# The D term of two state-space scans: from a matmul with a diagonal to a transpose of scaled rows, at every second state

## The reference

```
A_bar = exp(dt[t, d] * A[d, n])
h[t, d, n] = A_bar * h[t-1, d, n] + dt[t, d] * B[t, n] * x[t, d]
y[t, d] = sum over n of h[t, d, n] * C[t, n]  +  D[d] * x[t, d]
```

## Time and profile before

| What | us |
|---|---|
| median of 3 runs | 686.62 |
| lowest and highest run | 686.56, 692.63 |
| span of the profiled execution, first to last instruction | 657.3 |
| PE busy in the span | 602.7 (92%) |
| DVE busy | 530.2 (81%) |
| ACT busy | 513.7 (78%) |
| POOL busy | 429.1 (65%) |
| scan of layer 0, start of the first and of the last full recurrence | 49.35, 201.82 |
| scan of layer 1, the same | 282.08, 432.86 |

### The profile page before, as it was taken

One profiled execution on the slowest core, in us unless ns is written; L12 is line 12 of the kernel. 1 busy time (PEld: TensorE's weight loads), 2 busy tenths in 40 slices (PEclk: granted clock), 3 DMA queues, 4 the chain that ended last, 5 costly groups with the idle time before them and its releaser, 6 DMA issues.

```text
span 657.3 us, 12812 instructions
## 1 busy us (share of the span) xinstructions
PE 602.7 (92%) x4540; PEld 501.7 (76%) x4543; DVE 530.2 (81%) x899; ACT 513.7 (78%) x1182; POOL 429.1 (65%) x261
## 2 busy tenths in 40 slices
PE   5898999999996569799999999999999999999992
PEld 3388999999996434599999999989677555555662
DVE  6798999999998789989999999987863566555374
ACT  2999999999995798899999999967544665444335
POOL 0037999999999302479999999995004277777403
PEclk8979999999999699999999999999999999999997
DMA  7022333333331000044544454438112133333173
GB/s 198 6 67 65 112 112 105 108 109 114 103 110 32 2 0 7 19 147 134 180 128 153 145 159 155 147 91 274 43 64 65 33 97 97 97 99 96 56 265 128
DMA packets 41596, 67.78 MB, mean 103 GB/s; under 512 B 6688, under 2 KB 20928, under 8 KB 41536
## 3 DMA queue, kind: packets, MB, share of 16 engines
q1 hardware_dynamic: 37696, 56.50, 27.5%
q0 software_dynamic: 3840, 10.49, 5.1%
HBM read 57.28 MB, written 9.70 MB: 102 GB/s over the span
## 4 chain that ended last, share of the span: by engine, by line
PE 57%; DVE 14%; ACT 13%; POOL 8%; DMA 4%; issue 3%; DVEq 1%; SPq 0%; ACTq 0%; POOLq 0%
PE both L1383 16%; PE bank L1412 12%; POOL arena L1184 7%; PE both L1476 7%; PE both L1385 5%; PE both L1463 4%; PE bank L1483 4%; DMA arena<-w 2%; ACT rings L1045 2%; PE bank L1404 2%; DVE arena L658 2%; DVE st L443 1%; PE bank L1584 1%; ACT rings L923 1%; ACT tok_a L996 1%
## 5 line engine op out<-in xcount | busy, mean ns | idle before, releaser
L1184 POOL TENSOR_TENSOR arena<-arena,rings 128x1024 f32<-128x1024 f32 x126 | 296.8, 2375 | 17.5 <-DVE arena L658 13.4
L1383 PE MATMUL both<-rings,tok_a 128*128 128x128 f32 x1280 | 183.3, 277 | 3.6 <-DVE arena L658 2.2
L1383 PEld LDWEIGHTS both<-rings,tok_a 128*128 128x128 f32 x1280 | 164.6, 193 | 5.1 <-issue 2.9
L658 DVE TENSOR_TENSOR_SCAN arena<-rings,both 128x1024 f32<-128x1024 f32 x64 | 145.3, 2279 | 12.3 <-PE both L1385 4.5
L658 DVE TENSOR_TENSOR_SCAN arena<-late,both 128x1024 f32<-128x1024 f32 x62 | 140.7, 2278 | 7.1 <-PE both L1385 1.8
L1412 PE MATMUL bank<-ident,arena 128*128 128x128 f32 x1024 | 133.0, 273 | 2.8 <-POOL arena L1184 1.4
L1412 PEld LDWEIGHTS bank<-ident,arena 128*128 128x128 f32 x1024 | 115.7, 141 | 4.2 <-POOL arena L1184 1.9
L1045 ACT ACTIVATE rings<-ident,b_tok 128x128 f32<-128x128 f32 x320 | 106.6, 394 | 0.3
L1045 ACT ACTIVATE rings<-tok_a,b_tok 128x256 f32<-128x256 f32 x192 | 89.7, 500 | 0.0
L1385 PE MATMUL both<-ident,rings 128*128 128x128 f32 x384 | 84.0, 273 | 0.0
L1199 POOL TENSOR_TENSOR arena<-arena,feat_a 128x512 f32<-128x512 f32 x8 | 19.4, 2425 | 86.2 <-DVE arena L554 86.2
(11 more groups left out here) (233 smaller groups left out, 1045.9 us busy)
## 6 DMA issues: line engine op xcount, KB each, us to landing
rings<-c_rows SPq DMA_DIRECT2D x128, 256.0 KB, 3.2
w_sb<-w SPq DMA_DIRECT2D x18, 352.0 KB, 4.2
arena<-w SPq DMA_DIRECT2D x2, 2048.0 KB, 13.2
residual<-x SPq DMA_DIRECT2D x4, 512.0 KB, 5.8
x_rows<-tok_a SPq DMA_DIRECT2D x4, 512.0 KB, 2.6
tok_a<-y_tok SPq DMA_DIRECT2D x4, 512.0 KB, 6.3
w_sb<-y_tok SPq DMA_DIRECT2D x4, 512.0 KB, 7.0
out<-residual SPq DMA_DIRECT2D x8, 256.0 KB, 2.6
```

The source lines that it names most:

```text
L658: dve.tensor_tensor_scan(h_s, decay_s.rearrange("p h t -> p (h t)"), both[s % B_RING][:, :], 0.0, ALU.mult, ALU.add).then_inc(h_ready, 1)
L1184: pool.tensor_tensor(h_both, h_both, c_row, ALU.mult).then_inc(hc_ready, 1)
L1383: pe.matmul(o, tok_a[:, c, h * P:(h + 1) * P], v_ring[:, s % V_RING, j, 0:P], start=True, stop=True)
```

## The change

It has three parts.

1. The D term is no longer a matmul with a diagonal matrix. POOL scales `feat_a` by D in place, behind its u of each quarter (two tensor_scalar of 128 x 512 for each quarter, eight per layer), and PE turns the scaled rows into the sums by a transpose that accumulates. `d_diag` and its two DVE instructions go, with their waits. POOL waits for both halves of u of the quarter before it scales, since u is made from the same `feat_a`.
2. The eight D products of a batch stand at every second state (n = 1, 3, ..., 15) and no longer at n = 1 to 8.
3. `diagonals(s)` is 3 in even steps and 2 in odd ones, where it was 2 at the states 1 to 8 and 3 at the others. The number of product chunks over a layer is the same: 160 of 256.

```diff
-        d_diag = uT[:, 0, 0:H * P].rearrange("p (h d) -> p h d", h=H)
...
-        d_ready = sem("d_ready")
+        skip_ready = sem("skip_ready")
...
                 elif name == "dt":
-                    if q == Q - 1:
-                        dve.wait_ge(utr_copied, l * Q * 2 + 2)
-                        for h in range(H):
-                            dve.tensor_scalar(d_diag[:, h, :], ident[:, :], dskip_sb[l][:, h:h + 1], None, ALU.mult)\
-                               .then_inc(d_ready, 1)
                     settle()
...
                     pool.tensor_tensor(uT[:, H - 1, t], dtT[:, H - 1, t], feat_a[:, H - 1, t], ALU.mult).then_inc(u_ready, 1)
+                    if k % Q == 0:
+                        pool.wait_ge(ld_ssm[l], 32)
+                    pool.wait_ge(u0_ready, k + 1)
+                    pool.wait_ge(u_ready, k + 1)
+                    for h in range(H):
+                        pool.tensor_scalar(feat_a[:, h, t], feat_a[:, h, t], dskip_sb[l][:, h:h + 1], None, ALU.mult)\
+                            .then_inc(skip_ready, 1)
...
                     if s == 2:
-                        pe.wait_ge(d_ready, (l + 1) * H)
-                    if 1 <= n <= H * CQ:
-                        j, h = divmod(n - 1, H)
+                        pe.wait_ge(skip_ready, (l + 1) * BATCH * H)
+                    if n % 2 == 1:
+                        j, h = divmod(n // 2, H)
                         c = b * CQ + j
-                        pe.matmul(y_part(b, j, h), feat_a[:, h, c * P:(c + 1) * P], d_diag[:, h, :], start=False, stop=False,
-                                  skip_group_check=True)
+                        pe.matmul(y_part(b, j, h), feat_a[:, h, c * P:(c + 1) * P], ident[:, :], start=False, stop=False,
+                                  is_transpose=True, skip_group_check=True)
...
 def diagonals(s):
 
-    return 2 if 1 <= batch_state(s)[1] <= 2 * CQ else 3
+    return 3 - s % 2
```

## The result

The changed kernel took 684.9 us in the median of 17 runs (681.51 to 687.82), against 689.6 (686.5 to 694.51) for 17 runs of the kernel before beside them. The ratio is 0.992, with a 95% interval of 0.9899 to 0.9941. It is faster by 0.8%, some 5.5 us (the two medians alone are 4.7 apart), within the 1% that I called no change. The profiled execution took 685.0 us, with a span of 683.1, so 1.9 us lie around the span.

What follows compares the result with a forecast made beforehand. The scans were taken to hang mostly on PE, with ACT the next bound. Scan gains of 2.7 and 3.3 us less head slips of 1.2 and 1.8 gave 686.62 - 3.2 = 683.4 us, range 680.0 to 690.0.

Steps and rivals of the forecast that it cites:

- the rival in which the scalings hide: In the head, POOL's scalings run only in DVE's pauses and each u keeps its place: 680.4 us, chance 20%.
- one of the signs that I had named for being wrong: Wrong if a scaling takes well over 1.23 us, PE idles in the scan at old pace, or low clock grows 3.4.
- PE's price of a step: In the scan, PE needs 9.46 us over four steps, 2.365 a step in place of 2.43.
- ACT as the next bound: In the scan, ACT's work is only spread evenly, 4.74 us a pair or 2.37 a step, nearly PE's pace.
- The gain of the scans, 2.7 and 3.3: From first to last recurrence, layer 0 gets 2.7 us shorter and layer 1 3.3, together 6.0.
- `d_diag` credited with 0: In the head, removing DVE's two instructions, 1.48 us in layer 1 with 1.2 of it a wait, gains 0.
- A scaling at 0.48 to 1.23, taken as 0.85: In the head, one POOL scaling takes 0.85 us, between a write-only memset and a two-input product; 1.7 a quarter.
- Each scaling holds DVE up or is held up: In the head, a POOL scaling either stops DVE or waits for it, keeping the next u behind it in POOL's queue.
- The slip of layer 0, taken as 1.2: In layer 0's head, one or two scalings fall on DVE's chain and make ACT late: 0.85 to 1.7 us.
- The slip of layer 1, 0.85 to 2.6, taken as 1.8: In layer 1's head, scalings ahead of quarter 2's u delay PE, so the scan starts 1.8 us later.
- The scalings of quarter 3 at 0: They run under the first recurrence and end about when POOL's first product could start, so they cost 0.
- 29.3 us around the span: The median was taken to lie 29.3 us above the trace's span, 657.3 before and 654.1 forecast.

Runs made afterwards that it cites:

- the two halves: Against the kernel before: the D transpose and its scalings alone, ratio 0.9924; D products at every second state with 3 and 2 product chunks in turn alone, 0.9941.

## Why the prediction was right, and where its steps were not

The time forecast, 683.4 us, and its range of 680.0 to 690.0 hold the measured 684.9. The difference to the kernel before is what the prediction was about: 3.2 us forecast, 5.5 by the ratio (4.1 to 7.0 by its interval), 4.9 to 5.9 by the stages. Sign and class are right, and the size is short by some 2 us: it lies nearer to the rival in which the scalings hide (6.2) than to the forecast. That the medians agree to 1.5 us is in part luck: the kernel before took 689.6 in the longer comparison and not the 686.62 that I started from, and from there the forecast would have been 686.4. And one of the signs that I had named for being wrong was met: a scaling takes well over 1.23. The time held because what a scaling costs is not its length.

- **PE's price of a step:** right. 9.46 forecast for four steps, 9.49 measured; the steps are of four kinds (2.20, 2.43, 2.31, 2.55) and not of two in turn.
- **ACT as the next bound:** right. 4.74 forecast for a pair, 4.76 measured; the last recurrences wait for decays, and the kernels with two and three chunks throughout show each bound by itself.
- **The gain of the scans, 2.7 and 3.3:** 3.3 and 3.0 to 3.5. I took it from where ACT stood at the end, without saying how the loss comes about. The runs of the two halves show that 0.9 to 1.7 us of it in a layer was uneven steps, not the D product's price; the prediction called the old scheme balanced for PE and saw nothing in the spreading.
- **`d_diag` credited with 0:** right, by the kernel without scalings and the one that keeps it.
- **A scaling at 0.48 to 1.23, taken as 0.85:** wrong. It is 1.55 alone (two in a row took 3.11 in the kernel with twice the scalings, while DVE was idle) and about 2.0 beside DVE. The rows that I bounded it with, a memset and a two-input product, do not bound it. The Trainium skill (GPSIMD Engine Reference, engine selection) has one-input work near line rate, for which my estimate was 0.43, and it ranks it ahead of two-input work; the trace has it the other way round, 1.55 against 1.02.
- **Each scaling holds DVE up or is held up:** wrong for this form. Both go on, slower: a scaling stretches at most one of DVE's instructions, by 0.3 to 0.4 us, and mostly takes 1.8 to 2.3 itself. I had also read the 4.7 us of POOL's u as waiting, while 1.2 of it is its own work.
- **The slip of layer 0, taken as 1.2:** 1.5. I had it on DVE's chain as one or two scalings of 0.85, and it was DVE's chain, with four stretches of 0.3 to 0.4. But it reached the scan by the u of quarter 2 and by PE, for which the first recurrence waited; I had given PE's start room and looked at ACT. A scaling's length taken too small and its hold on DVE taken too large worked against each other, so that the size comes out near is partly luck.
- **The slip of layer 1, 0.85 to 2.6, taken as 1.8:** this is the term that was mis-sized. It measured 0.4. I had put POOL's late u of quarter 2 on PE's path there. PE's wait for it decided in layer 0, behind DVE's late adds; in layer 1 it came early, where it got into SBUF ahead of DVE for 1.65 in place of standing for 4.73. DVE's stretched chain filled its waits for ACT (1.92 and 0.68), of which the trace of before shows the first in part: 0.41 behind the 1.48 of `d_diag`. With 0.4 there and the rest as forecast the sum would have been 3.2 + 1.4 = 4.6, near the stages' 4.9 to 5.9.
- **The scalings of quarter 3 at 0:** right in its price and wrong in its reason. They end 2.9 us after the first product could have started, and PE waited 1.47 for it; that much is covered, and the 5.3 of the kernel with its scalings behind u is not.
- **29.3 us around the span:** wrong; it is 1.9. It did no harm because only differences were carried over.

## What to carry to other kernels

When an engine's step is made cheaper, work out the next engine's price first, and spread the dear and the cheap forms of a step evenly, so that both engines keep one pace; here that was worth 0.9 to 1.7 us a layer, beside 1.9 to 2.5 for the cheaper instruction. Work handed to another engine is paid for by what it does to that engine's neighbours and to what stands behind it, not by its busy time. In the heads here it cost what it stretched on VectorE, less the waits that absorbed it, wherever it stood in GpSimd's list. Do not pile it up ahead of the first instruction of a loop further than the loop's buffers let the other engines run on. An engine that looks free is not always a better home: DVE's scalings stood behind POOL's u. And compare the span of a trace with its own time before carrying a number from one to the other.

## What the runs showed of the hardware

- A GpSimd tensor_scalar of 128 x 512 float32, with D from a pointer for each partition, took 1.55 us, longer than the two-input form on the same data (1.02). Beside it one of VectorE's two-input instructions went from 0.68 to 1.09, where the two-input form of 1.02 cost VectorE 0.84.
- VectorE's own scaling of 128 x 512 took 1.30 to 1.40 us where it started while GpSimd's two-input product was running; a tensor_scalar of the same size in its own chain (L533) takes 0.41 with nothing beside it.
- The same kernel takes 688.03 and 687.76 us on two chips and 659.5 on a third, 4% apart. Two traces of it, with spans of 685.8 and 657.3, differ by 28.5 us in the mixture of experts, at a mean granted clock of 0.95 against 0.98. Why was not tried.
- The granted clock fell to 0.50 for 3.4 us behind a wait of 3.62 us by PE in the kernel with its scalings behind u; behind the wait of 1.47 in the kernel after, at the same place, it did not.
